# A recurrent cell and an attention block on one core: VectorE takes copies and sums of squares past the scan

## The reference, cut to what matters

```
def step(h, xt):                      # scanned over 256 steps
    m = concat([xt, h]) @ weight + bias
    g, c = sigmoid(m[:, :U] + 1.0), tanh(m[:, U:])
    return g * h + (1 - g) * c
x = x + scan(step, x)
q, k, v = (to_heads(plin(xm, w, b)) for w, b in (wq, wk, wv))
attn  = softmax(logmap0(q) @ logmap0(k).T / sqrt(HD))
out_h = expmap0(attn @ logmap0(v))
attn_out = plin(from_heads(out_h), w_o, b_o)
attn_t   = g_msa * logmap0(attn_out)          # needs norms of both
x1 = mobius_add(residual, expmap0(attn_t))
... layer norm, two linear layers, mobius_add ...
```

## Time and profile before

| | us |
|---|---|
| median of 3 runs | 455.86 |
| lowest and highest run | 455.79, 456.7 |
| the profiled execution, whole | 455.24 |
| its span, from the first to the last instruction | 453.4 |

### The profile page before, as it was taken

How to read it: one execution, slowest core, us unless ns; L and a number is a source line. 1 busy time by engine, 2 the same in 40 slices (tenths; PEclk the granted TensorE clock), 3 DMA queues, 4 the chain that set the end, 5 groups by cost and what they waited for, 6 DMA issues and landing times.

```text
span 453.4 us, 11610 instructions
## 1 busy us (share of the span) xinstructions
PE 343.0 (76%) x3768; PEld 215.6 (48%) x3768; DVE 344.5 (76%) x1973; ACT 275.8 (61%) x1031; POOL 71.4 (16%) x146
## 2 busy tenths in 40 slices
PE   4886897787647776647897988979689889767832
PEld 3633664455435454435554555536345446446410
DVE  3889866787999887899987888754932388699883
ACT  2445654455557445557566566646688888954951
POOL 1000000111000111000021000042300215266580
PEclk9999999999999999999999999986679989996958
DMA  6204800020000000000000000000000000000102
GB/s 182 66 1 105 177 2 1 3 48 2 1 1 2 2 0 2 1 2 1 2 1 3 0 4 0 3 2 3 1 2 3 1 3 3 1 3 0 25 1 69
DMA packets 9567, 8.28 MB, mean 18 GB/s; under 512 B 1282, under 2 KB 8212, under 8 KB 9508
## 3 DMA queue, kind: packets, MB, share of 16 engines
q1 hardware_dynamic: 8948, 7.28, 7.0%
q10 hardware_dynamic: 560, 0.27, 0.2%
HBM read 6.47 MB, written 1.08 MB: 17 GB/s over the span
## 4 chain that ended last, share of the span: by engine, by line
DVE 46%; PE 29%; ACT 13%; issue 7%; POOL 2%; DMA 1%; ACTq 0%; DVEq 0%; POOLq 0%
DVE guessed L1626 9%; DVE state L1626 8%; DVE sets L1647 5%; PE zb L830 5%; DVE rest L1645 5%; ACT sets L1316 4%; PE tb L964 3%; PE firsts L1135 3%; PE tb L774 3%; ACT prd L1480 2%; PE zb L1115 2%; ACT prd L1460 2%; PE zb L810 1%; PE firsts L1021 1%; PE tb L935 1%
## 5 line engine op out<-in xcount | busy, mean ns | idle before, releaser
L1316 ACT ACTIVATE sets<-zb 128x32 f32<-128x32 f32 x479 | 106.4, 228 | 110.5 <-PE zb L830 102.4
L830 PE MATMUL zb<-guessed,whh 128*128 128x8 f16 x960 | 64.3, 173 | 24.1 <-DVE guessed L1626 1.3
L1626 DVE TENSOR_TENSOR_SCAN state<-sets 128x32 f32<-128x32 f32 x256 | 57.0, 223 | 27.8 <-ACT sets L1316 25.7
L830 PE MATMUL zb<-rest,whh 128*128 128x8 f16 x480 | 51.5, 178 | 32.8 <-DVE rest L1645 31.7
L830 PEld LDWEIGHTS zb<-rest,whh 128*128 128x128 f16 x480 | 35.5, 112 | 80.5 <-DVE rest L1645 75.1
L1626 DVE TENSOR_TENSOR_SCAN guessed<-sets 128x32 f16<-128x32 f32 x255 | 57.4, 225 | 10.9 <-ACT sets L1316 2.8
L830 PEld LDWEIGHTS zb<-guessed,whh 128*128 128x128 f16 x960 | 44.2, 107 | 42.4 <-DVE guessed L1626 36.2
L1645 DVE TENSOR_TENSOR rest<-state,guessed 128x8 f16<-128x8 f32 x255 | 42.6, 167 | 8.7
L1480 ACT ACTIVATE prd<-zb 128x640 f32<-128x640 f32 x64 | 41.9, 710 | 5.8 <-PE zb L1115 5.1
L1647 DVE COPY sets<-state 128x32 f32<-128x32 f32 x255 | 44.7, 175 | 0.0
L635 POOL TENSOR_TENSOR stat<-mv 128x4 f32<-128x4 f32 x4 | 0.8, 203 | 229.2 <-DVE mv L1779 229.2
(11 more groups left out here) (370 smaller groups left out, 680.9 us busy)
## 6 DMA issues: line engine op xcount, KB each, us to landing
mod<-ada_rows SPq DMA_DIRECT2D x4, 768.0 KB, 11.0
resid<-in_x_dram SPq DMA_DIRECT2D x6, 128.0 KB, 3.0
ffz<-shift_rows SPq DMA_DIRECT2D x4, 131.0 KB, 3.1
out_dram<-state SPq DMA_DIRECT2D x8, 64.0 KB, 2.1
out_dram<-early SPq DMA_DIRECT2D x8, 64.0 KB, 2.1
yy<-in_L_cond_w_ada_dram SPq DMA_DIRECT2D x1, 384.0 KB
early<-in_L_cond_weight_dram SPq DMA_DIRECT2D x2, 128.0 KB
resid<-in_x_dram ACTq DMA_DIRECT2D x2, 128.0 KB, 3.6
```

The source lines that it names most:

```text
L830: return pe.matmul(bank[:, 256 * k + i:256 * k + i + NB], whh[:, half, k, :], h, start=False, stop=False, skip_group_check=True)
L1316: return act.activation(view(sets[:, n, 3:4], [39, 2], [38, 2], [4, NB]), view(bank[:, i:i + 1], [256, 2], [0, 2], [1, NB]), ACT.Tanh, sca ...
L1626: return dve.tensor_tensor_scan(dst, *scan_terms(n), 0.0, ALU.mult, ALU.add)
```

## The change

Only work past the scan moves, and only from ACT to DVE:

- The last chunk's four copies of the queries are on DVE, each right ahead of the copy of the same pair's keys, which needs no wait of its own any more.
- For the first and the second tail (`EARLY_TAILS`), DVE does the copy of `oT`, at the tick that ACT's copy had.
- For the same tails DVE does both sums of squares, where its dot `adot` stands. An instruction on DVE squares a 128x128 tile through two tensor inputs, and for the first of the two sums the projection is copied from PSUM to SBUF ahead of them, with a wait for the copy's end. `wo_sq` and `att_sq` are signalled from there.

The tables of ticks are as before. PE's, POOL's and SP's instructions stand as before.

```diff
+EARLY_TAILS = (0, 1)
@@ ACT, tokens
-                        order = ((high, 0), (high, 1), (queries, 0), (queries, 1), (high, 2), (high, 3),
-                                 (queries, 2), (queries, 3))
+                        order = ((high, 0), (high, 1), (high, 2), (high, 3))
@@ ACT, tail
                     for p, j in enumerate(pairs):
+                        if j in EARLY_TAILS:
+                            continue
                         yield from at_ticks(now, base + T["oevac"][p])
@@ DVE, tokens
+                    def queries(j, _):
+                        dve.wait_ge(stack_ps, NJ * c + j + 1)
+                        dve.tensor_copy(QT[:, j, :, P * c:P * c + P],
+                                        tb[:, j % 2, :].bitcast(F16)[:, 0:512]
+                                        .rearrange("p (g t) -> p g t", g=4)).then_inc(q_stack, 1)
                     def keys(j, _):
-                        dve.wait_ge(q_stack, NJ * c + j + 1)
...
-                        order = ((scale, 0), (scale, 1), (low, 0), (low, 1), (scale, 2), (scale, 3), (keys, 0),
-                                 (keys, 1), (low, 2), (low, 3), (keys, 2), (keys, 3))
+                        order = ((scale, 0), (scale, 1), (low, 0), (low, 1), (scale, 2), (scale, 3),
+                                 (queries, 0), (keys, 0), (queries, 1), (keys, 1), (low, 2), (low, 3),
+                                 (queries, 2), (keys, 2), (queries, 3), (keys, 3))
@@ DVE, tail
+                        if j in EARLY_TAILS:
+                            yield from at_ticks(now, base + T["oevac"][p])
+                            dve.wait_ge(oT_ps, j + 1)
+                            dve.tensor_copy(T_OT[j], of_bank(j, "oT")).then_inc(oT_sb, 1)
...
                         dve.wait_ge(att_m, j + 1)
+                        if j in EARLY_TAILS:
+                            settled(dve.tensor_copy(T_F[j], of_bank(j, "wo")))
+                            dots(j, lambda col: st_of("asq", 0, col), T_OT[j], T_F[j], T_F[j], wo_sq)
+                            dots(j, lambda col: st_of("asq", 1, col), T_R[j], T_M[j], T_M[j], att_sq)
```

## The result

| us | before | after |
|---|---|---|
| median of 4 runs each, same chip | 456.02 | **459.12** |
| lowest and highest | 455.79, 456.70 | 458.39, 459.51 |
| the profiled execution | 455.24 | 458.39 |
| its span | 453.4 | 456.6 |

The ratio is 1.0064, with a 95% interval of [1.0045, 1.0082] (the brackets behind a ratio mean this from here on). The kernel became slower by 3 us, where I forecast 455.1 and a range of 453.4 to 456.8. (In the kernel after, lines stand 1 to 16 further down: the save is L1964, the dots and squares L2021, line 2190 is L2206.)

What follows compares the result with a forecast made beforehand. ACT was taken to bound the first tail's stretch (355 to 361 us), DVE the later one (378 to 388). -0.65 - 0.10 = -0.75 us on 455.24 gave 454.5; the median, 0.62 above, 455.1, range 453.4 to 456.8.

Steps and rivals of the forecast that it cites:

- Part 1, the queries: Four query copies leave ACT for gaps on DVE: gain 0.65 us, as 0.25 at the second copy and 0.40 at the fourth.
- The 0.25 ahead of it: Second query copy, ahead of the diagonal stage's first exponentials at 331.22 us: gain 0.25 us, bounds 0 and 0.31.
- Part 2, the first tail: DVE takes the first tail's copy and squares, a 2.42 us block: its chain runs 1.87 us ahead, bounds 0.95 and 2.2.
- Part 3, the second tail: Second tail's work on DVE, up to 388 us, gives back the first tail's advance: of 1.87 us some 0.10 arrive.
- POOL's power: First tail's artanh power on POOL at 376.18; norm and clip factor queue behind it, holding line 2190 to about 0.10 us ahead.
- rival 3: PE's clock falls after PE idles about 1 us more between 378 and 388 us: adds 0 to 3.0, taken 1.0; chance 0.15.
- the copy of `oT`, 0.61: Second tail's copy, new on DVE between the first Möbius step and 388 us: charged 0.61 us to DVE's chain.

Runs made afterwards that it cites:

- queries_only: Kernel after with only the four query copies moved to DVE, no tail moved: 455.18 us, ratio 0.9978 to the kernel before.
- first_tail: Kernel after with queries and the first tail on DVE, the second tail left on ACT: 453.52 us, ratio 0.9938 to the kernel before.
- tails_only: Kernel after with both tails on DVE but the queries back on ACT: 458.53 us, all seven executions above 457.
- second_tail: Kernel after with the first tail back on ACT, so queries and second tail on DVE: median 458.24 us, one execution at 635.8 left aside.
- after_again: Kernel after run once more, unaltered: 458.28 us, four executions at 456.02 to 456.23 and eight at 458.01 to 459.84.
- copy_second: first_tail plus only the second tail's copy of `oT` on DVE: 456.56 us, six executions at 454.08 to 454.40, six at 458.72 to 460.67.
- fill_six: Kernel after with useless multiplications in TensorE's waits at 359.8, 363.6, 369.05 and three between 378 and 388 us: 454.97 us.
- fifth_early: Kernel after with the fifth save alone earlier, ahead of the copy of `oT`: 455.05 us, two of twelve executions at 458.96 and 459.02.
- two_early: Kernel after with saves 5 and 6 earlier in DVE's order: 455.37 us, none of 12 executions above 457.
- saves_early: Kernel after with saves 5, 6 and 7 earlier in DVE's order: 454.49 us, none of 12 above 457, two at 456.8.
- first_early_save: first_tail with the seventh save put ahead of four DVE instructions: 452.69 us, ratio 0.9926 to the kernel before.

## Why the prediction was wrong

Each save's start, from DVE's timeline, cuts the stage into pieces that can be compared between executions (us; the place of the first save moves by 2 us from one execution to another and is left out; "none" speaks of this stretch alone):

| profiled execution | save 1 to 5 | 5 to 6 | 6 to 7 | 7 to 8 | 8 to the end | fall, 355 to 400 us |
|---|---|---|---|---|---|---|
| before | 29.59 | 9.36 | 8.30 | 6.88 | 59.38 | 368 |
| queries_only | 29.16 | 8.80 | 8.31 | 6.89 | 59.46 | none |
| first_tail | 27.46 | 8.81 | 8.30 | 6.89 | 59.42 | none |
| tails_only | 28.48 | 9.90 | 8.77 | 8.66 | 59.40 | 389 |
| second_tail | 29.73 | 9.90 | 8.65 | 6.88 | 59.48 | none |
| after | 28.04 | 9.88 | 8.65 | **9.34** | **60.46** | 387 |
| after_again | 28.04 | **12.98** | 8.30 | 6.88 | 59.44 | 371 |
| copy_second | 28.05 | **14.40** | 8.31 | 6.87 | 59.40 | 370 |
| fill_six | 28.22 | 9.90 | 8.64 | 6.88 | 59.45 | none |

Point by point:

- **Part 1, the queries.** Forecast 0.65, of which 0.40 behind the first save. Measured there: 29.59 - 29.16 = 0.43, and 28.48 - 28.04 = 0.44 between tails_only and after. Right. The 0.25 ahead of it can't be told from this table and stays open.
- **Part 2, the first tail.** Forecast 1.87; measured 29.16 - 27.46 = 1.70 between queries_only and first_tail. Right, and all of it arrives at the end: 455.18 - 453.52 = 1.66 by the medians.
- **Part 3, the second tail.** Forecast 1.77 given back, 0.10 of gain left. Measured 2.0: second_tail against queries_only, (29.73 + 9.90 + 8.65) - (29.16 + 8.80 + 8.31) = 2.01, and 46.57 - 44.57 = 2.00 between after and first_tail. What I named (POOL's power, its norm right behind, the clip factor, line 2190) came as I said, but the price was too low: a net gain of 0.10 was in truth a net loss of 2.0 - 1.7 = 0.3. By the saves 0.59 of the 2.0 is the copy ahead of the fifth save (28.05 - 27.46, copy_second against first_tail). The forecast's size, 0.75 up to the seventh save, was met at 47.25 - 46.57 = 0.68, but by luck. Before had a fall at 368 us of its own, in the profile that I priced from (0.57 in the earlier trace rows), and it cost 9.36 - 8.80 = 0.56, which the new kernel did not pay in that profile. Without it 0.12 is left.
- **The step that failed**: "From 388 us on no instruction moves and every engine starts from there by the same amount; this stretch I price at nothing", together with rival 3, for which I took 1.0 us and a chance of 0.15. In the profiled execution after, the fall cost 9.34 - 6.88 = 2.46 us there, and 60.46 - 59.44 = 1.0 more came behind the eighth save; 3.5 us in all, against a forecast of 1.0 and a bound of 3.0. In after_again it cost 12.98 - 9.88 = 3.1, of which 0.35 came back by the seventh save. It is not one mishap in seven: both profiled executions have a fall here, and of the 16 executions of this kernel 12 were at 458.0 or more.
- **And the step under it**: in part 3 I charged "the copy of `oT`, 0.61" to DVE's own chain and to nobody else. Behind it on DVE stood the fifth save, and behind the save PE's values. So the copy became a wait of 0.68 us on TensorE, just behind three that stand there with the first tail alone (0.27, 0.47, 0.37 in first_tail). copy_second has that wait and nothing else of the second tail, and half of its executions are 5.9 us longer by the medians of the groups (460.0 against 454.1); none of first_tail's six is. fifth_early takes that wait away and adds 0.73 us to the one behind the sixth save, and ten of twelve executions are at 456.03 or below. So it matters where TensorE waits, not only how long. I wrote that PE would idle more between 378 and 388 us; the place where it mattered most was 369.

The forecast was one for a TensorE whose clock holds. fill_six comes nearest to that kernel, and its 454.97 us lies 0.13 from the forecast of 455.1. That closeness is luck in part. Beside the kernel before in its own batch (456.21) it gains 1.24 us, where I forecast 456.02 - 455.1 = 0.9 on the same footing; and from the first save on the two profiles differ by only 113.51 - 113.09 = 0.42, less than the 0.56 of the fall that the kernel before has at 368.

Shown by runs: the second tail brings the loss and the first does not; TensorE's waits behind DVE's saves make the costly falls possible (above 457 us are 12 of 16 executions of the kernel after, 0 of 8 with the waits filled in fill_six, 0 of 12 and 0 of 12 with the saves moved in two_early and saves_early, the last with two shorter losses); the wait that the copy ahead of the fifth save makes is the main one; the place of a fall differs between executions of one program. Not shown: what amount or order of waiting brings a fall. The kernel before waits longer between 356 and 370 us than the kernel after (3.21 against 2.63 us in the waits that the trace lists) and its fall there is short; second_tail's profiled execution has waits of 0.94, 0.44, 0.40 and 0.68 us in a row and no fall. Open too: why the fall at 368 us that the kernel before shows ends by 372 us, and those of the kernels with the added wait last 10 us or more, with TensorE busy throughout. And whether the waits of 378 to 388 us alone would slow many executions: two_early has waits as long there and no execution above 457 in 12, fifth_early two in 12.

The Trainium skill ("TensorE: Matmul & The Clock Gate", the section "A second HAM failure mode: psum-queue depth-cycling") tells of a kernel in which frequent short pauses of TensorE between groups of multiplications make the clock go to the lower level and back. The trace agrees, with waits of 0.27 to 0.68 us ahead of the fall at 369.6 in copy_second. The same page of the Trainium skill ("What's actually happening") has the point at which the clock rises moving from run to run of one kernel, by 0.5 us either way. Here it is a fall that moves, and by far more, from 387 to 371 us in one program.

## What to carry to other kernels

When work moves to another engine, list what is queued behind it there, and who waits for that: a copy of 0.6 us on VectorE ahead of the save of a PSUM bank became a wait on TensorE, and through the clock it cost 5.9 us in every second execution (copy_second). Look at TensorE's waits in the stretch ahead of a dense one as a whole, and where several short ones stand together, as here, give a fall more than a rival's chance of 0.15. The cheapest cure was order: putting the save ahead of work that can wait (fifth_early: one number, upper group from 12 of 16 to 2 of 12), and the best kernel moves only what fits (first_early_save, 452.69 us).

## What the runs showed of the hardware

- The granted clock can stay at the lower level while TensorE is busy all the time: 9.00 of 9.00 us at 0.50 (copy_second, 371 to 380), 8.00 of 8.00 at 0.50 (after, 388 to 396).
- One program had the fall at 387 us in one profiled execution and at 371 in the next, and 4 of 16 executions are 2 us shorter than the rest, for a reason that no profile of them shows. One profile shows one draw of this; the spread of the times and the mean granted clocks show the others.
- At the lower level the values took 1.27 in place of 0.74 us and the projection 2.08 in place of 1.16: factors of 1.7 and 1.8.
- A fall can begin inside a wait of TensorE (386.9 us in after, 369.6 in copy_second) and also with TensorE at work (370.7 in after_again, where PE is busy 14.00 of 14.00 us from 370 to 384).
- Useless multiplications in TensorE's waits cost next to nothing: save 1 to save 5 took 28.22 us in fill_six and 28.04 in after, so 0.18, and the pieces from save 5 to save 8 are the same to 0.02 where neither has a fall.
